# Edge build's first group with one loop for each half, and layer 3's first sums moved beside layer 2's last tiles

## What is computed

```python
# layer 0: sums over incoming edges, two products, layernorm
agg = segment_sum(h[j], i)                       # counts of edges times h
x  += layernorm(relu((1 + eps) * h + agg @ W1.T + b1) @ W2.T + b2)
# layer 1: 8-head attention over the edges, then a small feed-forward part
# layer 2: edge_weight softmax over each source, sums both ways, two products
# layer 3
summed = segment_sum(h[src], dst);  deg = segment_sum(1, dst)
x  += relu((summed / max(deg, 1)) @ W_l.T + b_l + h @ W_r.T)
```

## Time and profile before

| | us |
|---|---|
| three timed runs | 1068.70, 1071.51, 1072.47 |
| their median | 1071.51 |
| the profiled execution | 1071.2 |
| its span in the trace | 1069.4 |
| TensorE matmul busy in the span | 988.8 (92%) |
| VectorE, ScalarE, GpSimd busy | 603.2, 455.2, 171.0 |
| mean granted TensorE clock, share of full speed | 0.976 |

### The profile page before, as it was taken

How to read it: one execution, slowest core, us unless ns; L and a number is a source line. 1 busy time by engine, 2 the same in 40 slices (tenths; PEclk the granted TensorE clock), 3 DMA queues, 4 the chain that set the end, 5 groups by cost and what they waited for, 6 DMA issues and landing times.

```text
span 1069.4 us, 17224 instructions
## 1 busy us (share of the span) xinstructions
PE 988.8 (92%) x5934; PEld 688.8 (64%) x5934; DVE 603.2 (56%) x1730; ACT 455.2 (43%) x783; POOL 171.0 (16%) x194
## 2 busy tenths in 40 slices
PE   6977887799989999899999999999998999889998
PEld 3455665588634555588888888875555898568543
DVE  6878899833885001476666666674537415830133
ACT  5611365441644100565666666662336604730000
POOL 0000001012053000233333200004726203000000
PEclk9999889899989999899999999999999999999999
DMA  6002588886100010454554410017001025000011
GB/s 179 1 0 74 165 270 265 257 285 217 46 1 1 1 39 1 155 158 133 154 153 131 127 38 2 2 50 297 1 1 53 3 69 172 3 38 1 20 39 38
DMA packets 75083, 97.25 MB, mean 91 GB/s; under 512 B 7439, under 2 KB 63894, under 8 KB 75006
## 3 DMA queue, kind: packets, MB, share of 16 engines
q1 hardware_dynamic: 74846, 96.21, 28.5%
q0 software_dynamic: 160, 0.00, 0.0%
HBM read 58.41 MB, written 37.90 MB: 90 GB/s over the span
## 4 chain that ended last, share of the span: by engine, by line
PE 77%; DVE 11%; issue 7%; ACT 3%; DVEq 1%; DMA 0%; SPq 0%; ACTq 0%
PE PS L929 8%; PE PS L946 8%; PE PS L897 8%; PE PS L645 7%; PE PS L866 6%; PE PS L1107 4%; PE PS L765 4%; PE PS L617 3%; PE PS L707 3%; PE PS L1152 3%; PE PS L1156 3%; DVE HT L1307 3%; PE PS L852 3%; PE PS L1045 2%; PE PS L1072 2%
## 5 line engine op out<-in xcount | busy, mean ns | idle before, releaser
L645 PE MATMUL PS<-HT,R 125*128 125x313 bf16 x636 | 130.1, 346 | 34.0 <-DVE HT L1307 15.3
L1449 DVE CUSTOM_DVE_ANT_0 HT<-PS,CD 128x1250 f32<-128x1250 f32 (+1 forms) x80 | 116.4, 1455 | 65.7 <-issue 65.7
L645 PEld LDWEIGHTS PS<-HT,R 125*128 x636 | 95.4, 172 | 69.2 <-issue 58.3
L1818 ACT ACTIVATE HT<-HT,soft 128x1250 f32<-128x1250 f32 (+1 forms) x80 | 107.1, 1339 | 10.2 <-DVE soft L1452 3.1
L1798 ACT COPY R<-PS 128x512 f32<-128x512 f32 (+1 forms) x120 | 64.6, 572 | 98.5 <-PE PS L929 98.3
L929 PE MATMUL PS<-K,HT 128*128 128x128 f32 (+2 forms) x800 | 103.0, 276 | 0.9 <-ACT HT L1818 0.8
L897 PE MATMUL PS<-R 64*128 64x512 f32 (+3 forms) x480 | 97.0, 536 | 3.1 <-DVE soft L1449 3.1
L929 PEld LDWEIGHTS PS<-K,HT 128*128 128x128 f32 (+2 forms) x800 | 85.5, 141 | 16.9 <-issue 14.8
L946 PE MATMUL PS<-R 128*64 128x128 f32 (+2 forms) x1600 | 94.2, 273 | 0.1
L1699 ACT COPY X<-PS 128x626 f32<-128x626 f32 x80 | 52.3, 694 | 96.2 <-PE PS L645 96.2
L1325 DVE TENSOR_SCALAR HT<-BC 125x314 bf16<-125x314 f16 x316 | 78.1, 310 | 23.8 <-PE PS L645 16.9
(11 more groups left out here) (276 smaller groups left out, 1523.3 us busy)
## 6 DMA issues: line engine op xcount, KB each, us to landing
edge_parts<-X SPq DMA_DIRECT2D x160, 160.0 KB, 2.8
R<-edge_parts SPq DMA_DIRECT2D x60, 156.5 KB, 2.5
CD<-edge_sums SPq DMA_DIRECT2D x1, 6250.0 KB, 20.9
counts_r<-edge_parts SPq DMA_DIRECT2D x10, 469.5 KB, 3.9
BC<-edge_parts SPq DMA_DIRECT2D x30, 156.5 KB, 2.4
CD<-edge_parts SPq DMA_DIRECT2D x3, 1565.0 KB, 12.1
edge_sums<-R SPq DMA_DIRECT2D x20, 156.5 KB
R<-edge_parts SPq DMA_DIRECT2D x18, 155.5 KB, 2.4
```

The source lines that it names most:

```text
L645: return mm(bank(b0 + h, QUART), stat, hot, start=first, stop=True, skip_group_check=True)
L1449: ve.tensor_tensor_reduce(Pb[s][a][0:n], PS[0:n, a * N:(a + 1) * N], cd[0:n, t, :], 1.0, -3e38, ALU.add, ALU.max, soft[0:n, s, a:a + 1]).t ...
L1818: sc.activation(Pb[s][a][0:n], Pb[s][a][0:n], ACT.Exp, bias=soft[0:n, s, 2 + a:3 + a], accum_out=zsum[0:n, z + a:z + a + 1]).then_inc(sem( ...
```

## The change

It has two parts.

**Group 0 of the edge build.** In place of one loop over the four halves of group 0 there are four loops, one after the other; a pass of the loop of half h takes four chunks of this half, all into its bank. The trip count of half h is a quarter of its chunks beyond two, rounded up, and at least one. Group 0 has now 8 values in the table (4 offsets, 4 ends). A pass can reach two chunks beyond the last, so `dst_oh` gets two chunks of zeros (rows of 322 numbers; GpSimd clears them, and TensorE waits for that before group 0) and `key` two columns of -1. What lies behind `key` in its buffer, `low`, the parts of the weights and `iota` among it, moves by two words. The other 39 groups are as before.

**Layer 2's end and layer 3's start.** `rest_back` is transposed at the end of `turn_c(9)` (beside tile 5) and copied by VectorE right after its part of C; `sel_back` after tile 6 of the first block of sums (`slots_turned`), into banks 0 to 2, and copied at the end of VectorE's work on `h3_lo`. Block 0 uses banks 3 to 5 (`sum_bank`), and so on in turn. `sum_tile(0, 0)` and `sum_tile(0, 1)` stand after the l2b matmuls of tiles 8 and 9; the transposes of H are no longer in the l2b loop but in a loop of their own behind it, with `sum_tile(0, t)` ahead of `turn(t)` from t = 2. The rounded copies of H's tiles 0 to 3 and the clearing of `y_heavy` and `sel_t` go to GpSimd, the copies of tiles 4 to 9 stay on ScalarE and stand ahead of all its copies of transposes; `h3_lo` follows on VectorE from tile 7 of its loop on.

```diff
+HEAD = 2 * GH
+NT = NG + GH - 1
+PAD = 2
...
-H_LOW, H_Y = 15, 25
+H_LOW, H_SEL, H_Y = 15, 26, 26
+BY_POOL = 4
...
-        dst_oh = R0[:, 0:NC * P // 2].bitcast(BF16).rearrange("p (m c) -> p m c", m=P)
+        dst_oh = R0[:, 0:(NC + PAD) * P // 2].bitcast(BF16).rearrange("p (m c) -> p m c", m=P)
...
+        key_pad = BC[0:EC, 0:NC + PAD]
+        key = key_pad[:, 0:NC]
+        low = BC[0:EC, NC + PAD:NC + PAD + NC // 2].bitcast(F16)
...
+            def end(value, before):
+                return (value & ENDS).with_bounds(min_val=before + 2, max_val=(before + 1) * NC + 1)
+
+            a = HEAD - VALUES + VALUES * w if w else 0
+            v = nc.values_load_multi_w_load_instructions(winI[0:1, a:HEAD - VALUES + VALUES * (w + LOADS)], engines=(engine,))[1]
+            halves = [end(e, h) for h, e in enumerate(v[GH:HEAD])] if w == 0 else []
+            rows_of = [v[i:i + VALUES] for i in range(HEAD if w == 0 else 0, len(v), VALUES)]
+            groups = [(u[0:GH], end(u[GH], w + (w == 0) + k)) for k, u in enumerate(rows_of)]
+            return halves, ([(v[0:GH], halves[GH - 1])] if w == 0 else []) + groups
...
+        def first_fixed_chunk(d, m, q):
+
+            return bass.ds((d + m * GH + (q - FIX)).with_bounds(min_val=q, max_val=NC - FIX - 1 + q), 1)
+
+        def first_late_chunk(d, m, s):
+
+            return bass.ds((d + m * GH + s).with_bounds(min_val=FIX, max_val=NC + PAD - 1), 1)
...
-            return 2 * (0, 3, 1, 2)[t % 4]
+            return 2 * (2, 3, 1, 0)[t % 4]
+
+        def sum_bank(f):
+
+            return 3 * ((f + 1) % 2)
...
             pe.wait_ge(sem("win_table"), 1)
+            pe.wait_ge(sem("h_pool"), 1)
...
+                    chunk = fixed_chunk(d[h], n0, q) if w else first_fixed_chunk(d[h], ([1] + halves)[h], q)
...
+                def first_half(h, m):
+                    for s in range(GH):
+                        pe.wait_ge(sem("late_oh%d" % s), m)
+                        step(h, dst_oh[0:EC, :, first_late_chunk(d[h], m, s)][:, :, 0], late_oh[:, s, 0:QUART])\
+                            .then_inc(sem("late_used%d" % s), 1)
+
+                def all_halves(m):
                     for h in range(GH):
                         pe.wait_ge(sem("late_oh%d" % h), m)
                         step(h, dst_oh[0:EC, :, late_chunk(d[h], m)][:, :, 0], late_oh[:, h, 0:QUART])\
                             .then_inc(sem("late_used%d" % h), 1)
+
+                for h in range(GH):
+                    base(0, h)
+                if w == 0:
+                    for h in range(GH):
+                        with pe.Fori(([n0] + halves)[h], halves[h]) as m:
+                            first_half(h, m)
+                else:
+                    with pe.Fori(n0, n1) as m:
+                        all_halves(m)
...
+                    if t == T - 1 and j == T - 1:
+                        i = rest_turned()
                     if t in (BANK // P - 1, T - 1):
                         i.then_inc(sem("cs_ps"), 1)
+
+            def rest_turned():
+
+                pe.wait_ge(sem("l2_w_in"), 96)
+                for u in range(T):
+                    n = rows(u)
+                    o = 5 * BANK + 256 + u * SLOTS_H
+                    i = nc.tensor.transpose(PS[0:n, o:o + SLOTS_H], rest_back[:, u * P:u * P + n], ident[0:SLOTS_H, 0:SLOTS_H])
+                return i
 
             pe.wait_ge(sem("ws_ev"), T)
...
-                if t == 7:
-                    heavy_turned()
-
-            def heavy_turned():
-
-                pe.wait_ge(sem("l2_w_in"), 96)
-                pe.wait_ge(sem("cs_ev"), T)
-                pe.wait_ge(sem("cs_ev_dve"), T)
+                if t >= T - 2:
+                    sum_tile(0, t - (T - 2))
+
+            def slots_turned():
+
+                pe.wait_ge(sem("l2b_y"), T)
                 for u in range(T):
                     n = rows(u)
-                    nc.tensor.transpose(PS[0:SLOTS_H, 3 * BANK + u * P:3 * BANK + u * P + n], sel_back[0:n, u, :], ident[0:n, 0:n])
-                    o = 5 * BANK + 256 + u * SLOTS_H
-                    i = nc.tensor.transpose(PS[0:n, o:o + SLOTS_H], rest_back[:, u * P:u * P + n], ident[0:SLOTS_H, 0:SLOTS_H])
+                    i = nc.tensor.transpose(PS[0:SLOTS_H, u * P:u * P + n], sel_back[0:n, u, :], ident[0:n, 0:n])
                 i.then_inc(sem("heavy_ps"), 1)
...
+                if f == 0 and t == 0:
+                    pe.wait_ge(sem("cs_ev"), T)
+                    pe.wait_ge(sem("cs_ev_dve"), T)
+                    pe.wait_ge(sem("h_dve"), H_TURNED)
...
-            def first_sums(i):
-                if i == T - LAG:
-                    pe.wait_ge(sem("l2b_y"), T)
-                    pe.wait_ge(sem("h_dve"), H_TURNED)
-                for t in (range(0, i + 1) if i == T - LAG else [i]):
-                    sum_tile(0, t)
 
             pe.wait_ge(sem("bias_parts"), 2 * BIAS_STEPS)
             pe.wait_ge(sem("l2_w_in"), 96)
             node_tiles("l2b", [1], lambda q, k, t, n: g2t[:, t * P:t * P + n], lambda q, k: w2c[:, :], banks=3,
-                       bias=bias_parts, turned=h_block, ready="l3_h", then=first_sums, beside=rest_of_c)
+                       bias=bias_parts, beside=rest_of_c)
+            for t in range(T):
+                if t >= 2:
+                    sum_tile(0, t)
+                turn("l2b", t, h_block, KF, "l3_h")
+                if t == 6:
+                    slots_turned()
             pe.wait_ge(sem("l2b_ht"), T)
+            pe.wait_ge(sem("h_dve"), H_SEL)
...
+            link(ve.tensor_scalar(first_trips, bank(6)[0:1, 0:GH], 1.0 / GH, (1 - NC - 1.5) / GH, ALU.mult, ALU.add))
+            ve.tensor_scalar(trips[:, GH:], trips[:, GH:], -float(NC + FIX), 1.0, ALU.add, ALU.max)
+            link(ve.tensor_scalar(first_trips, first_trips, 0.75, ROUND, ALU.max, ALU.add))
+            link(ve.tensor_scalar(first_trips, first_trips, -ROUND, None, ALU.add))
+            ve.tensor_scalar(room[:, GH:], trips[:, GH:], -1.0, float(NC - FIX), ALU.mult, ALU.add)
+            link(ve.tensor_scalar(first_room, first_trips, -float(GH), float(NC - FIX), ALU.mult, ALU.add))
...
-                i = ve.tensor_tensor(dst_oh[0:EC, (q + 1) * 4 * SUB:(q + 2) * 4 * SUB, :],
-                                     dst_oh[0:EC, 0:4 * SUB, :],
+                i = ve.tensor_tensor(dst_oh[0:EC, (q + 1) * 4 * SUB:(q + 2) * 4 * SUB, 0:NC],
+                                     dst_oh[0:EC, 0:4 * SUB, 0:NC],
...
+                def first_half(h, m):
+                    for s in range(GH):
+                        dve.wait_ge(sem("late_used%d" % s), m)
+                        ve.tensor_scalar(late_oh[:, s, :], iota[0:EC, :], KEY * h, key_pad[:, first_late_chunk(d[h], m, s)],
+                                         ALU.add, ALU.is_equal)\
+                            .then_inc(sem("late_oh%d" % s), 1)
...
+                if j == T - 1:
+                    turned_rest = PS[:, 5 * BANK + 256:5 * BANK + 256 + T * SLOTS_H].rearrange("p (t r) -> p t r", t=T)
+                    ve.tensor_copy(cs_r[:, 0:T - 1, N:CW], turned_rest[:, 0:T - 1, :])
+                    ve.tensor_copy(cs_r[0:n, T - 1, N:CW], turned_rest[0:n, T - 1, :]).then_inc(sem("h_dve"), 1)
+
+            def rest_of_h(t):
+                n = rows(t)
+                if t < BY_POOL:
+                    dve.wait_ge(sem("h_pool"), 5 + t)
+                else:
+                    dve.wait_ge(sem("h_hi"), COPIED + 1 + t - BY_POOL)
+                ve.tensor_tensor(h3_lo[0:n, t, :], H[0:n, t, :], h3_hi[0:n, t, :], ALU.subtract).then_inc(sem("h_dve"), 1)
...
-                if t == T - LAGZ:
-                    dve.wait_ge(sem("cs_ps"), 2 * T)
-                    ve.memset(y_heavy[:, :].bitcast(F32), 0.0)
-                    link(ve.memset(sel_t[:, :].bitcast(F32), 0.0))
-                if t == 8:
-                    dve.wait_ge(sem("heavy_ps"), 3)
-                    turned_rest = PS[:, 5 * BANK + 256:5 * BANK + 256 + T * SLOTS_H].rearrange("p (t r) -> p t r", t=T)
-                    ve.tensor_copy(cs_r[:, 0:T - 1, N:CW], turned_rest[:, 0:T - 1, :])
-                    ve.tensor_copy(cs_r[0:rows(T - 1), T - 1, N:CW], turned_rest[0:rows(T - 1), T - 1, :])
-                    for p0 in (0, 32):
-                        i = ve.tensor_copy(sel_t[p0:p0 + SLOTS_H, :], PS[0:SLOTS_H, 3 * BANK:3 * BANK + N])
-                    i.then_inc(sem("h_dve"), 1)
-
-            for t in range(T):
-                n = rows(t)
-                dve.wait_ge(sem("h_hi"), COPIED + t + 1)
-                ve.tensor_tensor(h3_lo[0:n, t, :], H[0:n, t, :], h3_hi[0:n, t, :], ALU.subtract).then_inc(sem("h_dve"), 1)
+                if t >= 7:
+                    rest_of_h(t - 7)
+            for t in range(T - 6, T):
+                rest_of_h(t)
+            dve.wait_ge(sem("h_pool"), 5 + BY_POOL)
+            dve.wait_ge(sem("heavy_ps"), 3)
+            for p0 in (0, 32):
```

(72 more changed lines are left out.)

46 lines of the change are left out of this document (19 added, 27 removed).

## The result

| | before | after |
|---|---|---|
| median of the runs, us | 1070.77 | 1107.07 |
| lowest to highest | 1068.70 to 1072.47 | 1106.47 to 1109.28 |
| span of the profiled execution | 1069.4 | 1104.8 |

What follows compares the result with a forecast made beforehand. Waits between TensorE and VectorE were taken to bound group 0 and the seam of layers 2 and 3; 12.7 + 0.8 = 13.5 us less gave 1057.7, plus 0.3 for the median 1058.0, range 1055 to 1063.

Steps and rivals of the forecast that it cites:

- Group 0: Edge build's first group: 14 passes replace 25, each still 1.15 us, so 12.7 us less.
- Addresses and loop starts: Group 0's loops: an added address multiplication (3.1 us if exposed) and three loop starts (4.8 us if dear), both taken as nothing.
- rival B: Group 0's loops are dearer: exposed addresses and loop starts stalling on issue cost 3.1 to 4.8 us, total 1062; chance 0.14.
- The 16 matmuls at 85.87: After group 0's last pass, 16 matmuls in 3.29 us: taken to show a cheap loop exit, gain at most 1 us.
- The setup: Ahead of group 0: about eight more operations, about 1 us (up to 2.5), hidden under 2.55 and 4.1 us of cover.
- The whole 12.7 us passes on: Edge build after group 0: stores, copies and loads all move together, so the full 12.7 us gain reaches the end.
- The 1.61 us of issue: Wait ahead of 107.05, where a group starts by loading registers; used to bound three new loop starts at 4.8 us.
- the seam: Layer 2's end to layer 3's start: one 5.52 us gap becomes gaps of 3.0 and 2.4; 0.8 us less.
- C: Edge build's weight loads slow at stride 322 instead of 320; if doubled, 59 us more, total 1117; chance 0.03.
- The 2.4: TensorE's second gap between layers 2 and 3, in us: `turn(2)` waits for ScalarE's copy of `turn(0)` until 939.9.
- rival A: Layers 2 to 3: half clock after both gaps and tile 9's product stuck cost 1.7 us, total 1060.5; chance 0.12.
- my two bounds: GpSimd's four rounded copies, layer 2 to layer 3: 0.61 to 1.27 us each, ready before they are wanted.

## Why the prediction was wrong

**Group 0, right.** 14 passes instead of 25, at 1.15 us: forecast 12.7 less, measured 12.4 (28.9 to 16.5). Addresses and loop starts cost nothing that shows: rival B did not happen. (The 16 matmuls at 85.87 include the four of the last pass; that changes no term.) The setup stayed covered: TensorE starts group 0 at 57.00 (57.79 in the earlier trace rows), though VectorE waits 1.58 us on issue for its first load, now of 23 registers, instead of 0.81.

**"The whole 12.7 us passes on", the step that failed.** I followed the gain through transfers, copies and queues and took groups 1 to 39 to be as before because their loops are. Their loads were not: of the change to the table I costed the operations that write it and not the ones that read it, though the diff shows their start address move from VALUES w to VALUES w + 3. The 1.61 us of issue in the earlier trace rows was such a load. I said so, and used it only to bound what the new loops might cost, not to ask what the change does to the loads themselves. It was an aligned load, and no row that I had shows one off 16 bytes, so the size could not be foreseen; that a read of the table moves could. Nine loads at 5.4 us are the 48.2 us. The gain did not get lost on the way; a cost nearly four times as large was put beside it. With the one unused word the whole change measures 1056.8 against the 1058.0 forecast, partly by luck: the seam gives 1.2 us less than forecast, and groups 1 to 39 take 133.9 us instead of 135.1, 1.2 less.

**The rivals.** C has the right sign and place, something of the new layout of the build, but the wrong mechanism: weight loads at the stride of 322 take 156 ns, and the table alone, moved in the kernel before, makes a loss as large. C had 0.03, all of the chance of slower, and that was far too small: a change that moves buffers has more ways of being slower than the one I had named.

**The seam, right in what ends each gap and off by 1.2 us.** Forecast: gaps of 3.0 us (by `h_lo`) and 2.4 (by ScalarE's copy of `turn(0)`); measured 3.28 and 2.70. The 2.4 owes something to luck: its working puts H of tile 9 at 937.4, but the terms beside it, 935.7 and 1.47 - 0.69, give 936.5 and a gap of 1.5. In that place the trace has ScalarE's rounded copies of tiles 5 and 6, which start at 972.71 and take 1.13 us ahead of H of tile 9; the working does not name them. Forecast 0.8 less with one spell at half clock; both gaps were followed by one (granted clock 0.50 at 966 to 970 and at 978 to 980), and the stretch is 37.3 us against 36.9 before. That is rival A's mechanism at a quarter of its price.

```profile
966.00:968.00 2.00, 2.00 (x6) 0.50 0.00 0
...
978.00:980.00 2.00, 2.00 (x8) 0.50 0.04 8
```

Rows of TensorE alone in the changed kernel: length, busy, granted clock, DMA share, GB/s. The last wait, for the copy of the last transposes, is the 0.58 above where I had 0.7. `sel_t` and GpSimd's copies were hidden: VectorE's two copies end 989.4, before the second block at 991.7, and the four rounded copies took 2.29 us together, 0.57 each, a little below the cheaper of my two bounds.

## What to carry to other kernels

When a change alters the layout of a buffer, list who reads it, not only who writes it, and look at the start address of each read, register loads first. A wait that the profile puts down to "issue" and that comes at a fixed rhythm can be an instruction that the timeline leaves out: find what the program has once in that rhythm, and ask for the view of its source line. Here that view, of the changed kernel alone, would have shown loads of 7.1 us before any experiment. In strict queues, put nothing that has to wait ahead of what another engine needs; at the seam two such places, one on TensorE and one on ScalarE, held 7 us of 37.3 between them, and moving instructions alone won them back.

## What was not expected of the hardware

A load of registers from a row in SBUF costs 0.25 to 0.28 us more for each register when its start address is 4, 8 or 12 bytes off a multiple of 16: of the build, 5.4 to 5.6 us for a load of 20, against about 1.0 us for a whole aligned load of 10. The loads themselves take 7.0 to 7.2 us (median, VectorE) in place of 2.0. It hits both engines that load here, VectorE and TensorE (waits up to 6.5 and 7.9 us), and the busy times of the stretches don't show it. The price is not the same everywhere: the first load, ahead of the build, takes 4.74 us when 4 bytes off and 1.60 before, 3.1 more, and the nine later ones 6.2 to 7.9. What makes them dearer, why an address off 16 costs at all, and whether the limit is the same for other lengths than 10 and 20, no run here shows.
